# Second attention of a two-layer block: one context burst per couple of heads, single-tile output product, transposes four rounds behind

## What is computed

```python
q_c = rmsnorm(hidden_states @ w_qa, g_qa)
q = (q_c @ w_qb).reshape(b, s, NH, QK).transpose(0, 2, 1, 3)
k_c, k_rope = (kv[..., :KVR], kv[..., KVR:])      # KVR = 64
kst = (k_c @ w_kvb).reshape(b, s, NH, ND + VD).transpose(0, 2, 1, 3)
q_rope = q_rope * cos + rotate_half(q_rope) * sin
scores = jnp.einsum('bhqd,bhkd->bhqk', query, key_s) * scaling
attn = jax.nn.softmax(scores, axis=-1)
out = jnp.einsum('bhqk,bhkd->bhqd', attn, v)
out = out.transpose(0, 2, 1, 3).reshape(b, s, NH * VD)
return out @ w_o
```

## Time and profile before

| | us |
|---|---|
| median of 3 runs | 974.87 (971.03 to 976.77) |
| the profiled execution | 972.94 |
| its span, first to last instruction | 971.1 |
| busy in the span: TensorE | 832.6 (86%) |
| VectorE | 705.3 (73%) |
| ScalarE | 541.2 (56%) |
| GpSimd | 534.7 (55%) |

### The profile page before, as it was taken

One profiled execution on the slowest core, in us unless ns is written; L12 is line 12 of the kernel. 1 busy time (PEld: TensorE's weight loads), 2 busy tenths in 40 slices (PEclk: granted clock), 3 DMA queues, 4 the chain that ended last, 5 costly groups with the idle time before them and its releaser, 6 DMA issues. The chain is left out here.

```text
span 971.1 us, 15146 instructions
## 1 busy us (share of the span) xinstructions
PE 832.6 (86%) x4568; PEld 549.7 (57%) x4568; DVE 705.3 (73%) x1368; ACT 541.2 (56%) x1160; POOL 534.7 (55%) x470
## 2 busy tenths in 40 slices
PE   5678987379998894799999999997999999997376
PEld 0657776367775672456566565653665656554145
DVE  1649999754443562989889898988898989884453
ACT  2268777433331772666666666664666666663143
POOL 2043432211223223988889888985898889883013
PEclk9979999599999795999999999998999999999699
DMA  9430000274533340466666666664666666665101
GB/s 325 186 137 2 1 2 1 75 192 142 163 99 119 101 150 11 118 157 150 156 157 152 154 154 154 156 153 97 158 150 155 155 154 156 151 153 135 60 22 65
DMA packets 91617, 120.86 MB, mean 124 GB/s; under 512 B 30416, under 2 KB 41680, under 8 KB 91536
## 3 DMA queue, kind: packets, MB, share of 16 engines
q1 hardware_dynamic: 66960, 86.31, 32.1%
q10 hardware_dynamic: 24576, 33.59, 14.2%
HBM read 42.22 MB, written 2.10 MB: 46 GB/s over the span
## 5 line engine op out<-in xcount | busy, mean ns | idle before, releaser
L1453 DVE TENSOR_REDUCE nmax<-bank 128x1 f32<-128x512 f32 x256 | 174.1, 680 | 46.7 <-PE bank L1396 45.6
L1529 ACT ACTIVATE prob<-bank,nmax 128x512 f32<-128x512 f32 x172 | 118.3, 688 | 111.5 <-DVE nmax L1453 92.4
L1590 POOL TENSOR_TENSOR prob<-prob,rinv 128x512 f32<-128x512 f32 x129 | 132.5, 1041 | 39.6 <-DVE rinv L1461 37.7
L1394 PE MATMUL bank<-xk_hi,q_hi 128*128 128x512 f32 x256 | 113.2, 442 | 17.7 <-ACT prob L1529 12.9
L1469 DVE STREAM_TRANSPOSE blk<-prob 128x512 f32<-128x512 f32 x172 | 120.1, 698 | 6.2 <-ACT prob L1544 4.9
L1394 PEld LDWEIGHTS bank<-xk_hi,q_hi 128*128 128x128 f32 x256 | 48.3, 189 | 97.8 <-issue 53.6
L1395 PE MATMUL bank<-xk_lo,q_hi 128*128 128x512 f32 x256 | 101.6, 397 | 0.0
L1396 PE MATMUL bank<-xk_hi,q_lo 128*128 128x512 f32 x256 | 100.9, 394 | 0.0
L1585 POOL TENSOR_TENSOR q_lo<-stage_a,q_hi 128x512 fp32r<-128x512 f32 x64 | 82.0, 1281 | 23.2 <-ACT q_hi L1523 23.2
L1581 POOL TENSOR_TENSOR stage_a<-stage_a 128x512 f32<-128x512 f32 x64 | 82.7, 1292 | 7.0 <-DMA stage_a<-stage_a 6.2
L1529 ACT ACTIVATE stage_a<-bank,nmax 128x512 f32<-128x512 f32 x84 | 57.7, 687 | 48.2 <-DVE nmax L1453 41.4
(11 more groups left out here) (236 smaller groups left out, 2030.0 us busy)
## 6 DMA issues: line engine op xcount, KB each, us to landing
pT<-blk SPq DMA_DIRECT2D x256, 64.0 KB, 2.0
pT<-blk ACTq DMA_DIRECT2D x256, 64.0 KB, 2.2
raw_e<-blk SPq DMA_DIRECT2D x256, 64.0 KB, 2.1
raw_e<-blk ACTq DMA_DIRECT2D x256, 64.0 KB, 2.1
raw_e<-in_wo SPq DMA_DIRECT2D x16, 512.0 KB, 4.0
stage_a<-stage_a SPq DMA_DIRECT2D x128, 64.0 KB, 2.0
wmod<-in_wmod SPq DMA_DIRECT2D x6, 1024.0 KB, 10.9
stage_a<-in_wmod SPq DMA_DIRECT2D x12, 512.0 KB, 4.9
```

Of the source, the lines that this page charges most:

```text
L1394: pe.matmul(sbk, q_hi[:, u % 2, q], xk_hi[:, 2, ks], start=True, stop=False)
L1453: dve.tensor_reduce(nmax[:, s % RING:s % RING + 1], s_bank[s % 2][:, :], AX.X, ALU.max, negate=True).then_inc(max_done, 1)
L1529: act.activation(prob[s % RING], s_bank[s % 2][:, :], ACT.Exp, bias=nmax[:, s % RING:s % RING + 1], accum_out=rsum[:, s % RING:s % RING + ...
L1590: pool.tensor_tensor(prob[s % RING], prob[s % RING], bc(rinv[:, s % RING:s % RING + 1], [P, S]), ALU.mult).then_inc(norm_pool, 1)
```

## The change

Nothing is computed otherwise; the order of the same work is changed, together with the semaphore counts that follow from it.

- The context product of a couple stands in one burst of eight matmuls at r2 in place of two of four at r1 and r3.
- The output product stands in four single tiles at r4, r5, r6 and r7, after that step's scores (and projection), in place of two tiles at r6 and two at r7. Each tile signals by itself.
- The transposes stand four rounds behind the scores in place of three, and ahead of the reciprocals of their step. The moves on ScalarE follow one step later; its own normalization stands three steps behind in place of two.
- cT_hi stands at r2 on ScalarE (before: r3), cT_lo at r2 on VectorE (before: r4).
- SyncE's swap stands before the third move of a unit in place of the seventh.
- GpSimd's q_sum stands at the third round of a unit in place of the fourth.

```diff
-            TURN_LAG = 3
+            TURN_LAG = 4
+            ACT_NORM_LAG = 3
-            PV_AT = {1: (0, 1), 3: (2, 3)}
-            OUT_AT = {6: (0, 1), 7: (2, 3)}
+            PV_AT = 2
+            OUT_AT = {4: 0, 5: 1, 6: 2, 7: 3}
+            SWAP_AT = 2
...
-                            if n == 6 and u + 4 < UNITS:
+                            if n == SWAP_AT and u + 4 < UNITS:
                                 swap(u + 4)
...
-                        if (g := placed(PV_AT, s)) is not None:
-                            context(*g)
+                        if s % 8 == PV_AT and 0 <= s // 8 - 2 < COUPLES:
+                            context(s // 8 - 2)
...
+                        if TURN_LAG <= s < ROUNDS + TURN_LAG:
+                            turn(s - TURN_LAG)
                         if s % 2 == 0 and 2 <= s <= ROUNDS:
                             row_inv(s - 2)
-                        if TURN_LAG <= s < ROUNDS + TURN_LAG:
-                            turn(s - TURN_LAG)
                         if s % TPB in ROPE_AT and s // TPB + 2 < UNITS:
                             rotate(s // TPB + 2, ROPE_AT[s % TPB])
-                        if s % 8 == 4 and 0 <= s // 8 - 2 < COUPLES:
+                        if s % 8 == PV_AT and 0 <= s // 8 - 2 < COUPLES:
...
-                        if st == (ACT_NORM + 2) % TPB and 1 <= u <= UNITS:
-                            n = s - 2
+                        n = s - ACT_NORM_LAG
+                        if n % TPB == ACT_NORM and 0 <= n < ROUNDS:
...
-                        if s % 8 == 3 and 0 <= s // 8 - 2 < COUPLES:
+                        if s % 8 == PV_AT and 0 <= s // 8 - 2 < COUPLES:
...
-                        if st == 3 and u + 2 < UNITS:
+                        if st == 2 and u + 2 < UNITS:
                             q_sum(u + 2)
```

More of the change, by code:

```diff
@@ L1344, in move_ready @@
                 if u >= P_SLOTS:
-                    eng.wait_ge(pv_ps, 2 * (u // 2 - 1))
+                    eng.wait_ge(pv_ps, u // 2 - 1)
             def move(eng, u, g, jj):
@@ L1396, in scores, with context @@
                         pe.matmul(sbk, q_lo[:, u % 2, q], xk_hi[:, 2, ks], start=False, stop=True).then_inc(s_ps, 1)
-                    def context(j, kts):
+                    def context(j):
                         b = j // HP
-                        if kts[0] == 0:
-                            ge(pe, clo_done, j)
-                            for e in range(2):
-                                pT_ready(pe, 2 * j + e)
-                        for kt in kts:
+                        ge(pe, clo_done, j)
+                        for e in range(2):
+                            pT_ready(pe, 2 * j + e)
+                        for kt in range(TPB):
                             for e in range(2):
@@ L1410, in context, with project_out @@
                         mm.then_inc(pv_ps, 1)
-                    def project_out(j, tiles):
+                    def project_out(j, n):
                         b, p = j // HP, j % HP
-                        if tiles[0] == 0:
+                        if n == 0:
                             pe.wait_ge(clo_done, j + 1)
@@ L1418, in project_out @@
                                 ge(pe, x3_done, TPB * b)
-                        for n in tiles:
-                            ts = slice(n * P, (n + 1) * P)
-                            pe.matmul(o_bank[n][:, :], cT_hi[:, ts], b_hi[:, :], start=(p == 0), stop=False)
-                            pe.matmul(o_bank[n][:, :], cT_hi[:, ts], b_lo[:, :], start=False, stop=False)
-                            mm = pe.matmul(o_bank[n][:, :], cT_lo[:, ts], b_hi[:, :], start=False, stop=(p == HP - 1))
-                        mm.then_inc(o_ps, 1)
+                        ts = slice(n * P, (n + 1) * P)
+                        pe.matmul(o_bank[n][:, :], cT_hi[:, ts], b_hi[:, :], start=(p == 0), stop=False)
+                        pe.matmul(o_bank[n][:, :], cT_hi[:, ts], b_lo[:, :], start=False, stop=False)
+                        pe.matmul(o_bank[n][:, :], cT_lo[:, ts], b_hi[:, :], start=False, stop=(p == HP - 1)).then_inc(o_ps, 1)
                     project(0)
@@ L1516, in out_weights @@
                     def out_weights(j):
-                        ge(act, o_ps, 2 * j)
+                        ge(act, o_ps, TPB * j)
                         act.activation(b_hi[:, :], wb_all[:, j % HP, :], ACT.Copy).then_inc(bhi_done, 1)
@@ L1557, in _ @@
                             out_weights(s // 8 - 2)
-                        if s % 8 == 3 and 0 <= s // 8 - 2 < COUPLES:
+                        if s % 8 == PV_AT and 0 <= s // 8 - 2 < COUPLES:
                             j = s // 8 - 2
-                            act.wait_ge(pv_ps, 2 * (j + 1))
-                            ge(act, o_ps, 2 * j)
+                            act.wait_ge(pv_ps, j + 1)
+                            ge(act, o_ps, TPB * j)
                             act.activation(by_block(cT_hi[:, :]), ct_bank[:, :].rearrange("p (g t q) -> p g t q", g=QD, t=TPB),
```

2 lines of the change are left out of this document (1 added, 1 removed).

## The result

The changed kernel takes 983.27 us at the median (11 runs, 978.10 to 986.38), the kernel before 976.77 (11 runs on the same chip, 971.03 to 979.01). The ratio is 1.006, with a 95% interval of 1.0039 to 1.008: slower, where no difference was forecast, and 983.27 lies just above the range of 964 to 983. The profiled execution of the changed kernel took 978.10 us with a span of 976.2, so it is the fastest of the eleven, 5.1 us over the span of before.

What follows compares the result with a forecast made beforehand. TensorE was taken as dense before, and a ring through VectorE, ScalarE and TensorE as the bound after. Terms -4.4 (couples), -2.3 (batch change), +1.1 (first context) and +5.4 (end) gave -0.2 us: 974.7 us, range 964 to 983.

Steps and rivals of the forecast that it cites:

- The ring: Steady couples: VectorE's queue, ScalarE's exponential and TensorE's scores and burst form a closed chain of 15.29 us, against 15.44.
- Change of batch and end: Single terms outside the steady couples: -2.3 us where the batch changes, +5.4 us at the end of the stage.
- the order: End of the stage: last transpose behind couple 30's cT_lo, then the moves, so the last context starts later: +3.1 us.
- the slower bursts: End of the stage: TensorE's clock falls after idling about 3 us ahead of both contexts: 1.4 us twice, +2.8.
- VectorE's block: End of the stage: VectorE's closing block can start after one output tile in place of two: -0.5 us.
- The first context: Start of the stage: the first context stands one round later, +1.1 us, between 0 and 1.9.
- The clock: TensorE in the steady stretch: keeps full speed despite about 0.6 us idle in one place per couple.
- The moves: DMA moves on SyncE and ScalarE: last landings leave the context 0 to 0.5 us of cover; cost taken at zero.
- (b): Rival: SyncE's swap waits for the rotary of r4, delaying moves and context; +9.9 us, 984; chance 0.17.
- (a): Rival: VectorE's chain per couple is shorter, or the stage's end costs little; 965 to 970 us; chance 0.28.
- (c): Rival: TensorE stays the bound in steady couples, 14.4 us each; 945 us in all; chance 0.04.
- (d): Rival: TensorE's clock falls in every couple behind the idle time ahead of r2; +41 us, 1015; chance 0.03.

Runs made afterwards that it cites:

- e4: Changed kernel with two VectorE transposes put ahead of cT_lo, under the burst, and ScalarE's r2 normalization ahead of the exponential: 970.05 us, 0.9928 of the kernel before.
- e8: Kernel before with the whole context product in one burst at r1, nothing else changed: 1010.78 us, 1.0374 of the kernel before.
- e1: Changed kernel with cT_hi and cT_lo of couple 30 alone put back at r4: 977.91 us, 1.0002 of the kernel before.
- e5: e4 with ScalarE's moves of odd units at r2, r4, r5 and r6, their swap ahead of the fifth move: 964.87 us, 0.9895 of the kernel before.
- e6: e5 with couple 30's cT_hi and cT_lo two steps later, as in e1: 960.46 us, 0.9849 of the kernel before.
- e3: Changed kernel with SyncE's swap ahead of the seventh move again: 983.55 us, 1.0056 of the kernel before.
- e11: Changed kernel with ScalarE issuing 3, 2, 3 and 0 moves of odd units in r4 to r7: 977.96 us, 1.0035 of the kernel before.
- e7: Kernel before with ScalarE's moves one step later: 997.42 us, 1.0226 of the kernel before.
- e10: Changed kernel with transposes three rounds behind, ScalarE's lags as before and the reciprocal ahead of the transpose again: 983.76 us, 1.0089 of the kernel before.

## Why the prediction was wrong, step by step

**The ring: right, with one term mis-sized.** The idle time stands ahead of r2's scores, VectorE waits only ahead of cT_lo, no wait for cT_lo on TensorE, and the links are 4.33 (forecast 4.33), 8.30 (8.39), 1.01 (0.73 + 0.12), 0.84 (0.82) and 0.89 (0.90). The 0.12 for ScalarE's issues is 0.28, since two moves and their distance from the exponential of r7 set when that of r0 can start. 15.37 in place of 15.29. e4 and e8 show VectorE's queue as the cause from both sides. Against the measured 15.43 of before the couples give 1.7 us, not 4.4.

**Change of batch and end: right.** -2.7 (forecast -2.3). The end is 4.6 + 0.8 = +5.4, as forecast, and so are its terms: the order 3.0 (3.1), the slower bursts 1.6 and 1.4 (2.8 together), VectorE's block -0.6 (-0.5). e1 gives 5.0 of it back. The first context stands 0.4 us later behind the stage's first scores (forecast 1.1).

**The clock: right.** Granted clock 1.00 in the steady stretch with an idle time of 0.36 us ahead of the scores of r2 in each couple. The Trainium skill's rule on small idles between groups of matmuls ("TensorE: Matmul & The Clock Gate", section "A second HAM failure mode: psum-queue depth-cycling") did not show itself here. At the end the forecast 1.4 us behind each idle time were 1.6 and 1.4 (5.29 and 5.03 in place of 3.65). The first of the two was not certain: in e4 an idle time of 2.89 us ahead of context 30 left the burst at 3.65.

**The step that failed: "The moves", "I take the cost at zero".** I asked whether the landings of an ordinary couple come in time. They do, with 0.33 us, inside the forecast 0 to 0.5, and that costs nothing. What was put at nothing were the long issues, and the reading under it was wrong. "Up to 0.86" is the longest issue of one group, SyncE's moves into raw_e. The same view of before has, for the moves into pT:

```profile
L1349 SPq DMA_DIRECT2D pT<-blk x96: 507/592/2102, 455.8 to 624.2; - x96
L1349 ACTq DMA_DIRECT2D pT<-blk x96: 514/608/1866, 457.0 to 625.8; - x96
```

So issues of 2.10 us on SyncE and 1.87 on ScalarE stood there, ScalarE being an engine of the ring, and the forecast priced only a steady 0.12 for it. The trace has more: about every 31 us a 16 KB packet on the instruction queue runs beside issues of 1.2 to 2.2 us. From the first context on both kernels have 15 such packets; all 15 of the changed kernel have such an issue on SyncE or ScalarE, 13 of the kernel before. The DMA queues of the changed kernel, 455 to 458 us (packets, MB, share):

```profile
q1 hardware_dynamic: 144, 0.20, 27.1%
q10 hardware_dynamic: 113, 0.14, 18.9%
q8 instruction: 1, 0.02, 2.7%
```

In the kernel before the order had room for the long issues. SyncE's two issues there could take 2.79 us with no effect on the couple:

```profile
582.28 2.79 SPq L1349 DMA_DIRECT2D pT<-blk  x2
```

and one on ScalarE (833.12, 2.34 us for two), the worst case, cost its couple 0.46. In the changed kernel the ring runs through VectorE, ScalarE and TensorE without a free tenth, with two moves inside it between r7 and r0, and the landings only 0.33 us ahead of the context. Of the nine long couples four have a late exponential of r0 (4.5 us, with what landings add to them), three a late cT_hi (1.7), two a late landing alone (0.9). The three are ScalarE's issues again: in each a move of 1.9 to 2.0 us in r1 holds back the exponential of r2, and cT_hi stands behind that. So the step had the wrong path: not the landings but the issues, on ScalarE's way from one exponential to the next. +6.0 us, nothing of which was in the sum. The stage came out 0.4 - 1.7 + 6.0 - 2.7 - 0.5 + 5.4 = 6.9 us longer (6.8 unrounded), where 1.1 - 4.4 - 2.3 + 5.4 = -0.2 was forecast: of the 7 us between them 6.0 are the long couples and 2.7 the couple's median, and the small terms give 1.6 back.

**What stays open.** Only one execution of each kernel has a trace. That the long couples are of varying number fits the spread of 8 us, but that is argued, not shown. Whether the fetches do slow the issues or both follow from something else, no run here tells; they fall together. And the kernel before may have been lucky: eight of its 14 spacings between such packets are 30.6 to 30.9 us, two of its couples (30.86), so they meet the same place of the couple, a harmless one (5 issues over 1 us on ScalarE, 10 in the changed kernel, whose spacings go from 27.5 to 41.6). In the nine traces with the single burst at r2 other than e5 and e6 (whose couples spread) the excess goes with the number of these issues: 3 with 2.1 us, 5 with 4.2, 7 with 5.1 and 5.6, 10 with 7.0, 11 with 6.1 and 7.0, 12 with 7.3. So a comparison of the excess between two kernels is in part one of luck, and how much of the 6 us is luck was not tried.

**Rivals.** (b) named the right symptom, couples lengthened by what moves do, and 984 us, but its mechanism, the swap, is ruled out by e3. (a), (c) and (d) did not occur. The 945 of (c) counts the forecast's own gain twice: 29 x 0.89 below 974.7 is 949.

## What to carry to other kernels

When a change makes a ring out of what was a dense engine, sum the ring, and then ask of each link what its worst case in the trace is, not its median: a dense engine with work queued ahead absorbs a disturbance, a ring passes on what happens on its own links. Take that worst case from every group of the instruction in question: the one that looked harmless here stood beside two that were not. DMA issues on an engine that computes are links of its chain: put them where that engine has to wait anyway, and not in front of the operation that frees the next buffer. Look at the last item of a loop by itself: an order that is right in the steady state cost 3.7 us there and 1.4 more by a slower last burst, and one condition gave them back.

## What the hardware did that I had not expected

The issue of a DMA, 0.59 us at the median on SyncE and 0.61 on ScalarE, took 1.2 to 2.2 us on one or both of them about every 31 us, each time beside a 16 KB packet on the instruction queue; 8 KB packets on the other instruction queue went mostly without one. Three back-to-back issues between two exponentials set their distance at 2.0 us (517.02 to 519.03 in e11), two at 1.3 to 1.5, so each further issue costs about 0.6.

TensorE at the full clock did not fall for an idle time of 0.36 us in every couple. Longer idle times ahead of a context burst gave no single answer. Behind 2.99 us the burst took 5.29 us (granted clock 0.69), behind 2.89 us in e4 3.65 (1.00), behind 2.23 us 5.35 in e7 (0.68) and 3.65 in e10 (1.00). Behind 4.4 us it was slow each time, 4.97 to 6.12 us in six kernels. So the length of the idle time alone does not say whether the clock falls.
